# Attention scores by two row tiles and in one block of a step, two weight pieces converted earlier, keys projected once

## The reference

```python
x = x + xattn(layernorm(x), ctx, ctx, abundance, ...)      # 16 heads of 16, 64 keys per batch element
#   q = xn @ w_q.T + b_q ; k, v likewise from ctx
#   scores = q k^T / sqrt(16) + log(abundance) ; attn = softmax(scores) ; out = (attn v) @ w_o.T + b_o
x = x + ffn(layernorm(x), gate_w, expert_bias, w1, w2, w3)
#   scores = softmax(xn2 @ gate_w.T) ; the two best of scores + bias
#   out += silu(score * xn2 @ w1[e]) * (score * xn2 @ w3[e]) @ w2[e]   for each chosen expert e
```

## Time and profile before

| | us |
|---|---|
| median of 3 runs (lowest to highest) | 493.14 (491.72 to 495.26) |
| the profiled execution, its own time | 496.29 |
| span of the profiled execution | 494.5 |
| PE busy in the span | 410.3 (83%) |
| DVE busy | 267.1 (54%) |
| ACT busy | 195.1 (39%) |
| POOL busy | 222.7 (45%) |

### The profile page before, as it was taken

How to read it: one execution, slowest core, us unless ns; L and a number is a source line. 1 busy time by engine, 2 the same in 40 slices (tenths; PEclk the granted TensorE clock), 3 DMA queues, 4 the chain that set the end, 5 groups by cost and what they waited for, 6 DMA issues and landing times.

```text
span 494.5 us, 10564 instructions
## 1 busy us (share of the span) xinstructions
PE 410.3 (83%) x2969; PEld 310.3 (63%) x2970; DVE 267.1 (54%) x635; ACT 195.1 (39%) x351; POOL 222.7 (45%) x281
## 2 busy tenths in 40 slices
PE   4826998999998840148999999999999999999970
PEld 3613787877786730126777777777777777777740
DVE  2756566667674259824555555555555555555530
ACT  2256576686675344003333332333333333333310
POOL 5376355544446449032444444444444444444321
PEclk9877799999997655559999999999999999999985
DMA  6821343333263533010222222222222222232215
GB/s 201 267 90 61 100 165 116 103 111 90 97 191 112 179 109 95 1 33 13 44 44 43 36 40 40 37 43 43 43 43 42 33 43 36 39 43 43 33 21 180
DMA packets 29299, 38.35 MB, mean 78 GB/s; under 512 B 5205, under 2 KB 23906, under 8 KB 29250
## 3 DMA queue, kind: packets, MB, share of 16 engines
q1 hardware_dynamic: 21472, 27.60, 17.7%
q0 software_dynamic: 7488, 10.39, 13.1%
q10 hardware_dynamic: 322, 0.15, 0.1%
HBM read 28.62 MB, written 11.60 MB: 81 GB/s over the span
## 4 chain that ended last, share of the span: by engine, by line
PE 75%; DVE 8%; issue 4%; POOL 4%; ACT 3%; DMA 3%; POOLq 0%; SPq 0%; DVEq 0%; ACTq 0%
PE sc L1334 10%; PE sc L1335 10%; PE sc L1336 10%; PE ptps L1324 6%; PE bank L1357 6%; PE bank L1353 5%; PE bank L1199 5%; PE bank L1355 4%; PE bank L1268 3%; PE ptps L1244 3%; POOL w_lo L490 2%; PE bank L1306 2%; ACT w_hi L591 2%; PE bank L1257 1%; DMA w_hi<-n_L_xattn_in_proj_weight 1%
## 5 line engine op out<-in xcount | busy, mean ns | idle before, releaser
L567 POOL DMA_INDIRECT acc<-arena,put_now x39 | 62.5, 1603 | 113.4 <-DVE arena L1076 113.4
L1334 PE MATMUL sc<-w_hi,arena 128*128 x312 | 98.6, 316 | 1.0 <-DVE arena L1054 1.0
L1335 PE MATMUL sc<-w_hi,arena 128*128 x312 | 98.6, 316 | 0.0
L1336 PE MATMUL sc<-w_lo,arena 128*128 x312 | 98.5, 316 | 0.0
L490 POOL TENSOR_TENSOR w_lo<-stage_w,w_hi 128x1408 f16<-128x1408 f32 (+3 forms) x32 | 71.7, 2256 | 46.2 <-ACT w_hi L591 46.2
L1066 DVE SCALAR_TENSOR_TENSOR arena<-sc,slot_score,arena 128x352 f32<-128x352 f32 (+1 forms) x117 | 53.0, 481 | 66.9 <-ACT arena L735 66.9
L735 ACT ACTIVATE arena<-sc,slot_score 128x352 f32<-128x352 f32 x78 | 43.1, 553 | 90.6 <-PE sc L1336 90.6
L1353 PE MATMUL bank<-w_hi,arena 128*128 x234 | 64.1, 274 | 2.2 <-DVE arena L1081 2.2
L742 ACT ACTIVATE arena<-ptps 128x768 f16<-128x768 f32 x39 | 31.6, 810 | 83.5 <-PE ptps L1324 83.5
L1357 PE MATMUL bank<-w_lo,arena 128*128 x234 | 64.5, 275 | 0.0
L1079 DVE TENSOR_TENSOR arena<-ptps,arena 128x640 f16<-128x640 f32 x39 | 32.2, 824 | 44.4 <-ACT arena L742 44.4
(11 more groups left out here) (196 smaller groups left out, 714.0 us busy)
## 6 DMA issues: line engine op xcount, KB each, us to landing
stage_w<-in_L_ffn_w SPq DMA_DIRECT2D x16, 704.0 KB, 4.4
stage_w<-in_L_ffn_w SPq DMA_DIRECT2D x16, 256.0 KB, 2.9
stage_w<-in_L_ffn_w SPq DMA_DIRECT2D x32, 64.0 KB, 2.8
acc<-arena SPq DMA_DIRECT2D x16, 128.0 KB, 1.7
table<-xn SPq DMA_DIRECT2D x16, 128.0 KB, 1.8
arena<-in_x SPq DMA_DIRECT2D x2, 896.0 KB, 6.3
arena<-table,get_now POOLq DMA_INDIRECT x39, 2.8
acc<-arena,put_now POOLq DMA_INDIRECT x39, 3.8
```

The lines of the kernel that those rows point to most:

```text
L567: pool.indirect_dma_start(out=acc[:, :], out_offset=bass.IndirectOffsetOnAxis(ap=put_now[q][:, 0:1], axis=0), in_=y_sb[q], in_offset=None, ...
L1334: pe.matmul(ps[:, c, :], gT_hi[par][:, kk], w_hi[:, cols], start=k == 0, stop=False)
L1335: pe.matmul(ps[:, c, :], gT_lo[par][:, kk], w_hi[:, cols], start=False, stop=False)
L1336: ins = pe.matmul(ps[:, c, :], gT_hi[par][:, kk], w_lo[:, cols], start=False, stop=k == KD - 1)
```

## The change

- **Scores.** `scores_half` becomes `scores`: the two bias matmuls (512 columns each) come first; then each product of 128 rows by 512 columns is replaced by two of 64 rows by 256 columns (row groups 0 to 63 and 64 to 127; 4 heads each), whose outputs lie in different banks. A tile has 2 matmuls of 512 columns and 12 of 256 instead of 8 of 512. The heads are stored in another order in `sc_ps`; the bias and the value matmuls follow that order.
- **Place.** All scores of a step stand in one block, behind L1199, the row transposes and the L1217 transposes, and ahead of the output transposes. One semaphore increment is left, so both `maxima` wait for the whole block.
- **Keys.** The projection of the keys is of 128 columns instead of 256 (the copy is made by DVE's broadcast); the spread keys have 4 heads of 64 columns instead of 8.
- **Weight pieces.** SP loads pieces 0 and 1 ahead of the rest of x. ACT converts them between the prologue's copies, POOL ahead of `beta`.

Two conversions stand between the copies; two are left at the old place, behind the `v_blk` copies. The diff, cut to its core:

```diff
@@ -84,7 +84,8 @@
-        kb_hi, kb_lo = (take(2 * B * HS, F16).rearrange("p (c b n) -> p c b n", c=2, b=B) for _ in range(2))
+        HQ = HS // 2
+        kb_hi, kb_lo = (take(2 * B * HQ, F16).rearrange("p (c b n) -> p c b n", c=2, b=B) for _ in range(2))
...
@@ -358,7 +360,11 @@
-            for n in range(AHEAD):
+            for n in range(2):
+                load(n)
+            for b in range(B):
+                load_rest_of_x(b)
+            for n in range(2, AHEAD):
                 load(n)
...
@@ -478,24 +484,27 @@
...
+            for n in range(2):
+                piece_low(n)
+
             pool.wait_ge(s["bias_parts"], 1)
             for b in range(B):
...
             first_scales(*LN_GROUPS[1], 2)
             pool.wait_ge(s["kb_dve"], 8)
-            for n in range(AHEAD):
+            for n in range(2, AHEAD):
                 piece_low(n)
...
@@ -625,9 +634,11 @@
             tokens_high(0)
+            piece_high(0)
             act.wait_ge(s["wqT_ps"], 1)
             act.activation(wq_hi, sc_ps[0][:, 0:KD * D].rearrange("p (k n) -> p k n", k=KD), ACT.Copy)\
                 .then_inc(s["wq_hi_s"], 1)
+            piece_high(1)
             act.wait_ge(s["wvT_ps"], 1)
...
-            piece_high(0)
-            piece_high(1)
...
             for c in range(2):
                 dve.wait_ge(s["kT_ps"], c + 1)
-                dve.tensor_scalar(kT[:, c].rearrange("p b r s -> p (b r s)"), sc_ps[1][:, c * 512:c * 512 + B * P],
-                                  bias_qk[:, 2 + c:3 + c], HD ** -0.5, ALU.add, ALU.mult).then_inc(s["kT_sb"], 1)
+                dve.tensor_scalar(kT[:, c], sc_ps[1][:, c * 512:c * 512 + B * S2].rearrange("p (b s) -> p b s", b=B)
+                                  [:, :, None, :].broadcast_to([P, B, 2, S2]), bias_qk[:, 2 + c:3 + c], HD ** -0.5, ALU.add, ALU.mult).then_inc(s["kT_sb"], 1)
...
                 for c in range(2):
                     for dst, src in ((kb_hi, kT_hi), (kb_lo, kT_lo)):
-                        dve.tensor_tensor(dst[:, c, b, :].rearrange("p (h s) -> p h s", h=8),
-                                          src[:, c, b:b + 1, :].broadcast_to([P, 8, S2]),
-                                          head_mask[:, :, None].broadcast_to([P, 8, S2]), ALU.mult).then_inc(s["kb_dve"], 1)
+                        dve.tensor_tensor(dst[:, c, b, :].rearrange("p (h s) -> p h s", h=4),
+                                          src[:, c, b:b + 1, :].broadcast_to([P, 4, S2]),
+                                          half_mask[:, :, None].broadcast_to([P, 4, S2]), ALU.mult).then_inc(s["kb_dve"], 1)
...
@@ -894,7 +903,7 @@
 
                 def maxima(c):
 
-                    dve.wait_ge(s["s_ps"], 2 * tt + c + 1)
+                    dve.wait_ge(s["s_ps"], tt + 1)
                     hh = slice(c * H // 2, (c + 1) * H // 2)
                     dve.tensor_reduce(top[:, hh], sv[:, hh, :], AX.X, ALU.max).then_inc(s["smax"], 1)
...
-            def scores_half(par, c):
-
-                o = sc_ps[par][:, c * HS:(c + 1) * HS]
-                cc = slice(c * P, (c + 1) * P)
-                pe.matmul(o, qT_hi[par][:, cc], kb_hi[:, c, par, :], start=True, stop=False)
-                pe.matmul(o, qT_hi[par][:, cc], kb_lo[:, c, par, :], start=False, stop=False)
-                pe.matmul(o, qT_lo[par][:, cc], kb_hi[:, c, par, :], start=False, stop=False)
-                return pe.matmul(o, ones16[:, :], beta[:, par, c * HS:(c + 1) * HS], start=False, stop=True)
+            def scores(par):
+
+                for c in range(2):
+                    pe.matmul(sc_ps[par][:, c * HS:(c + 1) * HS], ones16[:, :], beta[:, par, c * HS:(c + 1) * HS],
+                              start=True, stop=False, skip_group_check=True)
+                for c in range(2):
+                    for q, kb, last in ((qT_hi, kb_hi, False), (qT_hi, kb_lo, False), (qT_lo, kb_hi, True)):
+                        for g in range(2):
+                            rows = slice(g * P // 2, (g + 1) * P // 2)
+                            at = g * HS + c * HQ
+                            ins = pe.matmul(sc_ps[par][:, at:at + HQ], q[par][rows, c * P:(c + 1) * P],
+                                            kb[rows, c, par, :], start=False, stop=last, skip_group_check=True)
+                return ins
...
             for c in range(2):
                 for k in range(KD):
-                    ins = pe.matmul(sc_ps[1][:, c * 512:c * 512 + B * P], wkT[:, k, c * P:(c + 1) * P],
-                                    ctxD[:, k].rearrange("p b r s -> p (b r s)"), start=k == 0, stop=k == KD - 1)
+                    ins = pe.matmul(sc_ps[1][:, c * 512:c * 512 + B * S2], wkT[:, k, c * P:(c + 1) * P],
+                                    ctxD[:, k, :, 0, :], start=k == 0, stop=k == KD - 1)
...
@@ -1175,6 +1190,36 @@
+                if here(t, 2):
+                    bt = tt - 2
...
+                    if here(t, 0):
+                        pe.wait_ge(s["q_lo_s"], tt + 1)
+                    for j in range(8):
+                        jv = j % 4 // 2 * 4 + j // 4 * 2 + j % 2
+                        ins = pe.matmul(bk7[:, jv * 2 * NOUT:(jv + 1) * 2 * NOUT], probT[par][:, j * P:(j + 1) * P],
+                                        v_blk[:, par, jv, :], start=True, stop=True)
+                    ins.then_inc(s["o_ps"], 1)
...
+                if here(t, -1):
...
+                    x_transpose(tt + 1, 1 - par)
+                if here(t, 4):
...
+                    for k in range(KD):
+                        ins = pe.transpose(pt_ps2[:, k * P:(k + 1) * P], xn2[par][:, k * P:(k + 1) * P], idt)
+                    ins.then_inc(s["x2t_ps"], 1)
                 if here(t, 0):
                     pe.wait_ge(s["q_lo_s"], tt + 1)
...
-                    scores_half(par, 0).then_inc(s["s_ps"], 1)
-                if here(t, 2):
...
-                    for j in range(8):
-                        ins = pe.matmul(bk7[:, j * 2 * NOUT:(j + 1) * 2 * NOUT], probT[par][:, j * P:(j + 1) * P],
-                                        v_blk[:, par, j, :], start=True, stop=True)
-                    ins.then_inc(s["o_ps"], 1)
...
-                if here(t, 0):
-                    scores_half(par, 1).then_inc(s["s_ps"], 1)
+                    scores(par).then_inc(s["s_ps"], 1)
```

More of the change, by code:

```diff
@@ L190, in xattn_moe @@
         head_mask = take(8)
+        half_mask = take(4)
         zero_rows = take(D)
@@ L325, in _, with load_rest_of_x @@
             sp.wait_ge(s["wkv_load"], 16)
-            for b in range(B):
+            def load_rest_of_x(b):
                 sp.dma_start(xs[:, b + 2:T:2, :], x[b, P:N, :].rearrange("(u p) d -> p u d", p=P))\
@@ L478, in _ @@
             assert n_c[0] == N_CONST
[L481 to L485, removed]
             def weights_low(number, staged, cols):
@@ L494, in piece_low @@
                 weights_low(n, stage[kind][buf], piece_columns(n))
+            for n in range(2):
+                piece_low(n)
+            pool.wait_ge(s["bias_parts"], 1)
+            for b in range(B):
+                pool.tensor_tensor(beta[:, b, :].rearrange("p (h s) -> p h s", h=H),
+                                   bias16[:, b * H:(b + 1) * H, None].broadcast_to([P, H, S2]),
+                                   key_diag[:, None, :].broadcast_to([P, H, S2]), ALU.mult).then_inc(s["beta_s"], 1)
             first_scales(*LN_GROUPS[1], 2)
             pool.wait_ge(s["kb_dve"], 8)
-            for n in range(AHEAD):
+            for n in range(2, AHEAD):
                 piece_low(n)
@@ L618, in queries_high @@
                 if not isinstance(tt, int) or tt >= 2:
-                    act.wait_ge(s["s_ps"], 2 * (tt - 1))
+                    act.wait_ge(s["s_ps"], tt - 1)
                 act.activation(qT_hi[par], bk7[:, 0:2 * P], ACT.Copy).then_inc(s["q_hi_s"], 1)
@@ L781, in _ @@
                     .then_inc(s["bq_s"], 1)
+            link(dve.tensor_tensor(half_mask[:, :], head_mask[:, 0:4], head_mask[:, 4:8], ALU.add))
             dve.wait_ge(s["ctxT_ps"], 1)
@@ L1158, in _ @@
                 for c in range(2):
-                    ins = pe.matmul(bk6[:, b * H + c * 8:b * H + (c + 1) * 8], kT[:, c, b].rearrange("p r s -> p (r s)"),
-                                    bq_blk[:, c, :], start=True, stop=True)
+                    o = bk6[:, b * H:(b + 1) * H].rearrange("p (g c h) -> p c g h", g=2, c=2)[:, c]
+                    ins = pe.matmul(o, kT[:, c, b].rearrange("p r s -> p (r s)"),
+                                    bq_blk[:, c, :].rearrange("p (g h) -> p g h", g=2), start=True, stop=True)
             ins.then_inc(s["bias_ps"], 1)
@@ L1177, in step @@
                 tt = 2 * u + par
-                if here(t, 0):
-                    pe.wait_ge(s["q_lo_s"], tt + 1)
-                    if t is None or t >= 2:
-                        pe.wait_ge(s["ssub"], tt - 1)
-                    elif t == 0:
-                        pe.wait_ge(s["kb_dve"], 4)
-                        pe.wait_ge(s["beta_s"], 1)
```

(17 more changed lines are left out.)

## The result

| | before | after |
|---|---|---|
| median of 4 runs (lowest to highest), us | 492.81 (491.72 to 495.26) | 517.8 (515.5 to 522.52) |
| ratio, 95% interval | | 1.051 (1.042 to 1.061) |
| profiled execution, its own time; span | 496.29; 494.5 | 519.88; 518.0 |
| PE busy, mean granted clock | 410.3, 0.898 | 416.3, 0.867 |
| first gather of the expert stage | 213.20 | 237.09 |

The direction was forecast, the size was not: 502 was predicted, and 517.8 lies just outside the range. The first gather comes 23.9 us later and the whole execution takes 23.6 us longer: all of the loss lies ahead of the expert stage. Where the runs of one kernel lie more than 1.5% apart, a ratio here is taken from the shorter ones, and the text gives the spread.

A forecast was written before the change was run, and what follows sets the result against it. It took PE to bound the steady attention steps, and a chain of waits the start. Its terms, -8.5 + 3.0 + 2.4 + 9.4 - 1.6 + 4 = +8.7 us, gave 505.0 in the profiled execution, median 502, range 490 to 517.

The forecast's parts named there:

- The start (-8.5): Step 1's scores come 6.0 to 10.5 us earlier through earlier weight pieces and less key work; taken as -8.5 us.
- Steps 1 and 2 (+3.0): The first two steps after step 0 get the same later maxima, 2 x 1.5 us.
- The block (1.2 us: All scores of a tile on PE take 1.2 us instead of 1.72, the row-group pairs overlapping, with 0.1 for switching.
- rival c: Row-group pairs run serially (+8 us), or the start gains only 3 us (+5.5): median 507 to 510; chance 0.14.
- The place: Scores in one block delay DVE's maxima and PE's output transposes: PE idles about 2 us, a step takes 8.75 us.
- X + 3.7: Output transposes start 3.7 us after X, where value matmuls end and row transposes start; before, 1.43 us after.
- steps 6 to 13: Eight steady attention steps of 8.75 us: 70.0 us against 60.62 before, +9.4.
- steps 14 and 15: Last attention steps, 8.75 us and an estimated 8.0: 16.75 us against 18.38 before, -1.6.
- The clock (+4): Gaps of 2 us bring the low clock for about a tenth of 12 steps' time, 10 us, half lost: +4 us.
- upper bound of 78 us: The clock term's upper bound: all 6.5 us of PE work doubled in each of 12 steps.
- Rival (d): Clock falls last a step or more: three low stretches costing 20 us instead of 4, median 518; chance 0.14.
- rival (a): The clock holds, all other terms as forecast: 501.0 us in the profiled execution, median 498; chance 0.18.

The follow-up runs named there:

- experiment 3: The kernel before with only the start changed (pieces 0 and 1 in the prologue, keys projected once): 489.13 us, ratio 0.992.
- experiment 7: The changed kernel with seven useless matmuls of 512 columns ahead of the output transposes: 501.86 us, ratio 1.015.
- experiment 4: The changed kernel with row-group scores in two parts at the two old places instead of one block: 487.54 us, ratio 0.989.
- experiment 9: The changed kernel with three useless matmuls of 512 columns ahead of the output transposes: 503.61 us, ratio 1.020.
- experiment 6: The changed kernel with each tile's bias matmuls made five times instead of twice, ahead of the gap: 526.4 us.
- experiment 5: The changed kernel with whole-array scores again (8 matmuls of 512 columns, 8 heads), still in one block: median 515.9 us.
- experiment 2: The kernel before with only the place changed, its whole-array halves in one block at the new place: 518.05 us, ratio 1.041.
- experiment 10: The changed kernel with five useless matmuls of 512 columns ahead of the output transposes: 499.85 us, ratio 1.012.
- experiment 1: The changed kernel with both maxima moved behind tokens_low on DVE: 487.6 us, ratio 0.984.
- 8: The changed kernel with whole-array scores in one block and both maxima behind tokens_low on DVE: 488.54 us, ratio 0.989.

## Why the prediction was wrong in size

**The start (-8.5).** The scores of step 1 came 6.9 us earlier, inside the bounds of 6.0 to 10.5. The upper bound is not the sum of its parts as stated: 6.0 and 5.4 make 11.4. The 1.9 us of the halved projection came nearly whole (2.00 instead of 3.75 us), the 1.2 of the spreading did not (4.07 instead of 2.49), and last came ACT's two conversions at the old place, which the prediction had not counted. By itself the start is a gain of 4.5 us in the medians of experiment 3.

**Steps 1 and 2 (+3.0).** From 31.76 to 54.19 are 22.43 us against 18.46 before: +4.0. The mean granted clock was 0.52 there (31.76 to 54.19), and 0.72 in the same steps before (38.67 to 57.13), so part of this term is the clock's too.

**The block (1.2 us, rival c).** Right. The two bias matmuls take 0.53 us instead of 0.43 and the twelve 0.76 instead of 0.65 (experiment 7's rows): the pairs overlap (one after the other, twelve would take 12 x 0.108 = 1.30). The rest, 0.10 and 0.11, I read as the price of each change between whole array and row groups: in experiment 4 it is the same, 0.32 instead of 0.215 and 0.43 instead of 0.32, with half the columns and half the matmuls. The Trainium skill ("TensorEngine Tiling (Array Packing)", Tiling Modes, Key Properties) says that a change of mode drains the TensorE; the trace agrees, with 0.21 us for both where I had allowed 0.1 in all.

**The place (step 8.75 us, X + 3.7, gap of 2 us).** Right: 8.66, X + 3.74 and 1.91. In experiment 7, where the clock holds, steps 6 to 14 take 147.63 - 78.65 = 68.98 us (forecast 70.0), and from step 3 to step 16 it is 165.57 - 53.28 = 112.29. The prediction's own terms without the clock give 25.8 + 70.0 + 16.75 = 112.55. That this agrees to 0.3 us is partly luck: steps 6 to 13 are 1.0 us too long in the forecast, and steps 14 and 15 (17.94 us in experiment 7) 1.2 too short.

**The clock (+4): the step that failed.** From step 3 to 16 the kernel after takes 184.49 - 54.19 = 130.3 us. Less 112.3, that is 18.0 us for the clock, over four times the 4 that I took. I had written "about a tenth of the time, 10 us of low clock, half lost", which would make 5 and not 4; it was a fall in 11 of 13 steps, ten of them of 3.4 us, and the last, in step 15, lasting to 193. The price of a fall could have been foreseen in kind (half of what runs at the low clock), but the number of falls was a guess from a single one in step 15. My upper bound of 78 us shows that I knew the term to be open; yet no row stands behind the tenth, "498 to 507 by the bounds of its terms" leaves that bound out, and the range ended at 517, below the 518 of rival (d). The only ground for a clock that holds was that it held before, in steps with short gaps, which says nothing of gaps of 1.9 us.

The terms not of the clock sum to +4.7, 501.0 in the profiled execution, median 498: rival (a). Experiment 7 has a median of 501.9 for just that, the rest being the start, which is worth 4.5 and not 8.5 in the medians. In the profiled executions the sum is -6.9 (start) + 4.0 (steps 1 and 2) + 27.9 (steps 3 to 15, 130.3 against 102.4) - 1.1 (from there to the first gather) = +23.9. Rival (d), 518, had the size right and the form wrong: not three long stretches, but ten short ones and a long one in step 15, where the clock had been low before as well.

The Trainium skill ("TensorE: Matmul & The Clock Gate", A second HAM failure mode: psum-queue depth-cycling) describes a kernel in which frequent short idle times between groups of matmuls make the clock go back and forth, so that the cost lies between the bursts. The trace agrees: gaps of 1.9 us in a PE that is busy 6.7 of 8.7 us, and 16 us lost. I weighed that page's part on transposes instead; in experiments 7 and 9 the same transposes stand at the same place, and the clock holds.

**What stays open.** Which gaps bring a fall. Gaps of 1.83 to 1.91 us brought one in nearly every step of the kernel after, in 8 of 12 steps of experiment 6, in one step between 54 and 150 in the profiled run of 5 and in none of experiment 2 between 86 and 184. That these falls need an idle gap is shown (7, 9, 10), and that its length matters; what else decides is not. Two things in the traces were not followed up. One is when the gap comes: the falls begin at 59.9, 70.1 and 80.4 and then every 10.24 us from 107.7 to 179.4 in the kernel after, and in experiment 6 (63.4 to 176.1) always 10.24 or 20.48 us apart. The other is the kind of matmul ahead of it. With the whole array (5) the shortest run, 508.4, is about what the profiled one (511.4, one fall) gives without its fall, and at 1.6 to 1.7 us a fall the longest, 521.1, has about eight more (an estimate; neither run has a trace). So the medians 517.8 and 515.9 look alike, but the kernel after pays more for the clock and less for the scores.

That the steps of 7.56 us in experiment 1 end on one chain (POOL's `nmr`, ACT's `xn2T`, the transposes of the exponentials) was read in its trace and not tried. In 8 PE comes to these transposes at the same point nearly without a wait, and experiment 4 has steps of that length without this wait at all.

## What to carry to other kernels

Before work is joined into one block, look who reads its first part: a reader that stands in an in-order queue ahead of a short chain holds up the whole chain, and here one line moved on DVE turned 517.8 us into 487.6. A wait on PE that comes back in every step can have two prices, its own length (12.7 us here) and what the clock does behind it (15.9 us); useless matmuls in the wait tell one from the other. A saving on the busiest engine counts only if nothing else ends the step: row groups save 0.43 us a tile, and experiments 1 and 8 are equal within 0.2%, so that the best versions here (1 and 4, 487.5 us) owe most of their gain to the start.

An engine's work moved to an idle place can slow its neighbour: POOL's two subtractions made DVE's spreading of 4 heads take 4.07 us instead of 1.42.

## What the runs showed of the hardware that was not expected

- Idle gaps of 1.83 to 1.91 us, once a step, are enough to bring TensorE from 2.4 to 1.2 GHz, for 3.4 us each time in steps 3 to 14, beginning at most 0.9 us after PE has started again (at 80.4, where the gap ended at 79.59; at 107.7, where it ended at 107.06). Gaps of 1.08 to 1.16 us at the same distance did so in none of these steps (experiment 9).
- The same kernel on the same chip took 508.4 and 521.1 us (experiment 5), the long runs at the lower granted clock (0.883 and 0.899 against 0.909 and 0.912). With the gap filled the spread was 1.2 us (experiment 7), but with five useless matmuls it was 5.1 (experiment 10): a wide spread is a reason to look at the clock, and no proof.
- Matmuls of 64 rows by 256 columns in two row groups, into two banks, run in pairs: twelve in 0.76 us, 0.11 of it over six times 0.108.
